# A state-space scan with a mixture of experts beside it: every second quad of scaled inputs kept in an accumulation bank

## The chip, the core and the metric

The kernel runs on one core of a Trainium2 chip. The metric is the time of one execution on the device, in microseconds (us), lower is better. Two runs of the kernel before stand beside each other in what follows: 1683.84 and 1686.05 us, with a median of 1684.94 us.

The engines are TensorE (PE, with its weight loads as PEld), VectorE (DVE), ScalarE (ACT), GpSimd (POOL) and the queue that issues most DMAs (SP). Each works through its own list of instructions in order; semaphores are what one waits for from another.

## The reference

`x` is 4 sequences of 1024 steps with 256 channels. After a layer norm two branches run on the same rows: a recurrent scan with 16 states for each channel, and a mixture of 8 experts (top 2, 1280 rows each at most) whose output gates the scan's. The scan is what matters here:

```
xn = layernorm(x)
dt = soft_clamp(softplus(xn @ Wdt.T + bdt), 0.001, 0.1, 0.5)
B, C = xn @ WB.T, xn @ WC.T
A = -exp(soft_clamp(A_log, -5, 5, 0.5))
dA = exp(soft_clamp(dt[..., None] * A, -8, 8, 0.5))      # decays
dB = dt[..., None] * B[:, :, None, :]
def step(h, ...):
    h = dAt * h + dBt * xt[..., None]                    # decayed state + scaled input
    h_norm = sqrt(sum(h * h, over all channels and states))
    h = h * min(20 / h_norm, 1)
    y = einsum(h, Ct) + Dp * xt
s = scan(step)                                           # 1024 steps, one after the other
out = x + s * silu(moe(xn))
```

## The kernel before

The state of one step is a tile of 128 partitions by 128 columns: a partition holds one of 4 sequences, 2 halves of the channels and 16 states, a column one of 128 channels. VectorE does the 1024 steps one after the other. The other engines prepare what a step needs, and do the mixture of experts in what time they have left.

**A step on VectorE** has seven instructions, here in the order in which they stand: `vv` = state times decay (L722); `mx`, the maximum with 1 of the square of the last norm (L725); the sum of `vv` times the scaled input (L728, a custom reduction, in the trace CUSTOM_DVE with a short accumulator read behind it); the sum of `vv` squared (L736, the same); the sum of both over the partitions (L740); the new state `hr`, which is `vv` times the last scale `sv` plus the scaled input (L751); and the next squared norm out of the sums and the scale (L755). Here and there one longer instruction of another chain (L618, L624, L641) stands between L740 and L751.

**GpSimd** raises `mx` to the power -1/2 (L531), which gives `sv`. L531 waits for L725 of the same step, and L751 waits for L531. After every 16th step GpSimd also multiplies 16 columns of scales (L538).

**Quads and blocks.** Work that prepares steps is done for a quad, which is 4 steps; 4 quads are a block (16 steps), and 4 blocks are a half (64 steps, 16 quads). Quads are numbered from 0 to 255. For quad q TensorE transposes four tiles of decays into one accumulation bank (L1170, `ps[0]` for even quads and `ps[1]` for odd ones), then spreads four tiles of inputs into another (L1176, always `ps[2]`), and behind them puts that quad's share of the experts' matmuls (L1188 up, L1204 down, L1115 turns). ScalarE copies the decays out to the ring `da` in SBUF (L952), writes the four inputs, scaled, to the ring `ur` in SBUF (L959, four instructions), then evicts the experts' results (L972, L976, L983) and computes the next half's decays (L858, L864) and the next halves' rates (L817 to L828).

Both rings have 32 slots, that is 8 quads. So ScalarE may be up to 8 quads ahead of VectorE; what holds it there is a wait at each block's start for the end of the block before the last (L942, on `q_ready`). VectorE, in the last step of a quad and ahead of L736, waits until the inputs of the next quad are written (`u_done`).

What each engine does in a quad is written out in the loops over `blk` and `q`; no scheduler changes the order. At a half's border ScalarE has far more to do than elsewhere: in the last quad of a half two decay exponentials (L864, 128x2048 each), in the first quad of the next half the windows of scales (L913), two more decay exponentials, and the softplus of a half that is still to come (L817 to L824).

## Time and profile before

| | |
|---|---|
| median of 2 runs | 1684.94 us (1683.84 to 1686.05) |
| span of the profiled execution | 1682.3 us |
| DVE busy | 1549.9 us, 92% |
| PE busy | 1305.2 us, 78% (PEld 1145.4 us) |
| ACT busy | 1211.1 us, 72% |
| POOL busy | 769.9 us, 46% |
| granted TensorE clock, mean | 0.874 of full speed |

The span goes from the first to the last instruction of the profiled execution. The page gives no time of that execution beside it; the two timed runs are 1.5 and 3.8 us longer than the span, which is what lies around it. The scan begins some 80 us after the start and its last step ends near 1657 us. From 350 to 1480 us the experts' matmuls run beside it.

### The profile page before, as it was taken

The numbers are of one execution on the slowest core, as the hardware profiler recorded it, in microseconds if no ns is written. First come the engines' busy times: TensorE is split into PE (matmuls) and PEld (weight loads), VectorE is DVE, ScalarE is ACT, GpSimd is POOL, SyncE is SP. The second block draws the span as 40 slices with busy tenths as digits, with TensorE's granted clock in tenths as the row PEclk, the third lists the DMA queues.
The fourth block names the chain that finished last, engine by engine and source line by source line (L and its number), as shares of the span: only waits on it lengthen the run. The fifth ranks groups of instructions, "written<-read, shape, count | busy, mean of one in ns | idle before, by whom it ended". The sixth has DMA issues, their size and how long they took to land.

```text
span 1682.3 us, 33906 instructions
## 1 busy us (share of the span) xinstructions
PE 1305.2 (78%) x9356; PEld 1145.4 (68%) x9356; DVE 1549.9 (92%) x9454; ACT 1211.1 (72%) x3142; POOL 769.9 (46%) x1254
## 2 busy tenths in 40 slices
PE   5864524398979898998989798898979799945661
PEld 5753424387868787787878687797868688834551
DVE  6688888899999999999999999999999989987788
ACT  3695737468877887868787877878777777947551
POOL 3156666543434444443434444343434334468852
PEclk8576767699989999999999999898999999967885
DMA  9941111210111021011002002011101210012245
GB/s 332 338 138 44 45 41 45 84 44 25 50 52 39 25 77 33 18 56 57 27 27 87 25 29 74 25 39 43 57 19 35 66 32 21 20 39 75 73 135 204
DMA packets 95532, 113.28 MB, mean 67 GB/s; under 512 B 8432, under 2 KB 85360, under 8 KB 95344
## 3 DMA queue, kind: packets, MB, share of 16 engines
q1 hardware_dynamic: 87696, 94.13, 17.4%
q0 software_dynamic: 6144, 16.79, 3.1%
q8 instruction: 74, 1.21, 0.3%
q14 instruction: 114, 0.93, 0.2%
q10 hardware_dynamic: 1504, 0.22, 0.1%
HBM read 60.91 MB, written 50.20 MB: 66 GB/s over the span
## 4 chain that ended last, share of the span: by engine, by line
PE 51%; ACT 15%; DVE 14%; POOL 7%; issue 7%; DMA 4%; SPq 1%; POOLq 0%; ACTq 0%; DVEq 0%
PE ps L1204 14%; PE ps L1188 13%; PE ps L1176 9%; PE ps L1170 5%; ACT arena L864 4%; POOL arena L531 4%; DVE arena L751 3%; POOL xg L511 3%; PE ps L1154 3%; PE ps L1138 3%; DVE arena L722 2%; DVE arena L728 2%; ACT arena L858 2%; DVE arena L740 2%; ACT arena L959 2%
## 5 line engine op out<-in xcount | busy, mean ns | idle before, releaser
L531 POOL TENSOR_TENSOR arena<-arena,neghalf 128x1 f32<-128x1 f32 x1025 | 591.3, 577 | 831.6 <-DVE arena L725 759.9
L751 DVE SCALAR_TENSOR_TENSOR arena<-arena 128x128 f32<-128x128 f32 x1024 | 362.6, 354 | 55.8 <-POOL arena L531 55.7
L1176 PE MATMUL ps<-arena,pick 128*128 128x128 f32 x2048 | 302.5, 295 | 48.7 <-ACT arena L959 28.3
L1188 PE MATMUL ps<-arena,wf 128*128 128x256 f32 x1280 | 309.6, 393 | 21.9 <-ACT arena L972 13.8
L1176 PEld LDWEIGHTS ps<-arena,pick 128*128 128x128 f32 x2048 | 279.3, 211 | 62.4 <-ACT arena L959 47.6
L959 ACT ACTIVATE arena<-ps,arena 128x128 f32<-128x128 f32 x1024 | 291.4, 376 | 30.5 <-PE ps L1176 28.8
L736 DVE CUSTOM_DVE_ANT_0 arena<-arena 128x128 f32<-128x128 f32 x1024 | 294.3, 287 | 8.0 <-PE ps L1138 6.5
L1204 PE MATMUL ps<-wp,arena 128*128 128x256 f32 x1280 | 297.3, 386 | 5.0 <-issue 2.7
L728 DVE CUSTOM_DVE_ANT_0 arena<-arena 128x128 f32<-128x128 f32 x1024 | 299.0, 292 | 0.0
L722 DVE TENSOR_TENSOR arena<-arena 128x128 f32<-128x128 f32 x1024 | 290.7, 284 | 0.0
L740 DVE TRANSPOSE_TENSOR_REDUCE arena<-arena 128x2 f32<-128x64 f32 x1024 | 251.3, 245 | 35.5
L1188 PEld LDWEIGHTS ps<-arena,wf 128*128 128x128 f32 x1280 | 245.1, 198 | 55.4 <-ACT arena L972 14.8
L858 ACT ACTIVATE arena<-arena,a16c,a 128x256 f32<-128x256 f32 x512 | 278.7, 609 | 0.1
L1204 PEld LDWEIGHTS ps<-wp,arena 128*128 128x128 f32 x1280 | 243.0, 195 | 36.7 <-issue 2.9
L1170 PE MATMUL ps<-ident,arena 128*128 128x128 f32 x1024 | 209.3, 331 | 59.6 <-ACT arena L864 58.8
L1170 PEld LDWEIGHTS ps<-ident,arena 128*128 128x128 f32 x1024 | 179.7, 244 | 89.0 <-ACT arena L864 64.8
L755 DVE TENSOR_TENSOR_SCAN arena<-arena 128x2 f32<-128x2 f32 x1024 | 221.1, 216 | 0.0
L952 ACT ACTIVATE arena<-ps 128x512 f32<-128x512 f32 x256 | 152.2, 595 | 70.8 <-PE ps L1170 61.4
L725 DVE TENSOR_SCALAR arena<-arena 128x1 f32<-128x1 f32 x1024 | 150.3, 147 | 0.0
L972 ACT ACTIVATE arena<-ps 128x512 f32<-128x512 f32 x160 | 95.4, 608 | 66.7 <-PE ps L1188 64.4
L913 ACT ACTIVATE arena<-arena,winmask 128x16 f32<-128x16 f32 x520 | 110.9, 316 | 21.2 <-POOL arena L538 21.0
L864 ACT ACTIVATE arena<-arena 128x2048 f32<-128x2048 f32 x64 | 119.0, 1907 | 0.2
(145 smaller groups left out, 1292.6 us busy)
## 6 DMA issues: line engine op xcount, KB each, us to landing
xg<-zeros SPq DMA_DIRECT2D x10, 1024.0 KB, 9.6
xrow<-xg SPq DMA_DIRECT2D x40, 256.0 KB, 2.8
yg<-arena SPq DMA_DIRECT2D x40, 256.0 KB, 2.2
arena<-in_x SPq DMA_DIRECT2D x16, 512.0 KB, 9.5
wf<-in_c_fc SPq DMA_DIRECT2D x8, 1024.0 KB, 5.0
wp<-in_c_proj SPq DMA_DIRECT2D x8, 1024.0 KB, 5.9
arena<-dx SPq DMA_DIRECT2D x66, 64.0 KB
ys<-arena SPq DMA_DIRECT2D x66, 64.0 KB
```

The costliest lines, as they stand in the source:

```text
L531: g.tensor_tensor(sv[:, slot, 1:2], mx, neghalf[:, 0:1], ALU.pow).then_inc(s_ready, 1)
L722: v.tensor_tensor(vv, hr[:, before, :], da[:, slot, :], ALU.mult).then_inc(v_ready, 1)
L728: v.tensor_tensor_reduce(out=junk[:, 0, :], in0=vv, in1=ur[:, slot, :], scale=2.0 / CLAMP ** 2, scalar=0.0, op0=ALU.mult, op1=ALU.add, acc ...
L736: v.tensor_tensor_reduce(out=junk[:, 1, :], in0=vv, in1=vv, scale=1.0 / CLAMP ** 2, scalar=0.0, op0=ALU.mult, op1=ALU.add, accum_out=ac[:, ...
L740: v.tensor_reduce(out=terms[:, slot, 0:2], in_=ac.unsqueeze(2).broadcast_to([P, 2, 32]), axis=AX.X, op=ALU.add, apply_transpose=True).then ...
L751: v.scalar_tensor_tensor(hr[:, slot, :], vv, sv[:, before, 1:2], ur[:, slot, :], ALU.mult, ALU.add)\
L858: last = a.activation(dst[:, :, k, n_, :], src[:, :, k, :], ACT.Tanh, scale=a16[:, c:c + 1], bias=a16c[:, c:c + 1])
L959: last = a.activation(ur[:, t + j, :], ps[2][:, j * P:(j + 1) * P], ACT.Copy, scale=terms[:, t + j, 3:4])
L1170: last = t.transpose(ps[q % 2][:, j * P:(j + 1) * P], tanhb[:, f, :, s], ident[:, :])
L1176: last = t.matmul(ps[2][:, j * P:(j + 1) * P], pick[:, q * QUAD + j, :], xin, start=True, stop=True)
L1188: last = t.matmul(ps[4 + j % 2][:, c * TS:(c + 1) * TS], wf[:, k, (2 * j + c) * P:(2 * j + c + 1) * P], xt[:, k, :], start=k == 0, stop=k ...
L1204: last = t.matmul(ps[7][:, j * D:(j + 1) * D], hid[:, k, j * P:(j + 1) * P], wp[:, k, :], start=k == 0, stop=k == FC - 1)
```

## The change

The scaled inputs of the even quads (slots 0 to 3, 8 to 11 and so on of the ring) are no longer written to `ur` in SBUF. ScalarE writes them into the accumulation bank `ps[1]`, and VectorE's L728 and L751 read them there. Odd quads stay in `ur`. Since the bank holds one quad, ScalarE waits, ahead of the first of the four writes of an even quad, until VectorE has done the last step of the even quad before it, two quads back: `h_ready` at `QUAD * quad + BLK - 3`, which is L751 of step 4q - 5. The bank is taken from the decays, which now all go through `ps[0]`; TensorE's transposes of a quad therefore wait until ScalarE has copied out the decays of the quad just before (earlier: two before). The lists of all five engines have the same instructions in the same order as before; what differs is where operands lie and two waits.

```diff
@@ names @@
+        def inputs_at(slot):
+
+            j = slot % QUAD
+            return ur[:, slot, :] if slot // QUAD % 2 else ps[1][:, j * P:(j + 1) * P]
@@ VectorE, each step @@
-                    v.tensor_tensor_reduce(out=junk[:, 0, :], in0=vv, in1=ur[:, slot, :], scale=2.0 / CLAMP ** 2, scalar=0.0,
+                    v.tensor_tensor_reduce(out=junk[:, 0, :], in0=vv, in1=inputs_at(slot), scale=2.0 / CLAMP ** 2, scalar=0.0,
...
-                    v.scalar_tensor_tensor(hr[:, slot, :], vv, sv[:, before, 1:2], ur[:, slot, :], ALU.mult, ALU.add)\
+                    v.scalar_tensor_tensor(hr[:, slot, :], vv, sv[:, before, 1:2], inputs_at(slot), ALU.mult, ALU.add)\
@@ ScalarE, before the loop @@
-            act.sem_inc(da_done, 2)
+            act.sem_inc(da_done, 1)
@@ ScalarE, each quad @@
-                    a.activation(da[:, t:t + QUAD, :].rearrange("p t d -> p (t d)"), ps[q % 2][:, :], ACT.Copy)\
+                    a.activation(da[:, t:t + QUAD, :].rearrange("p t d -> p (t d)"), ps[0][:, :], ACT.Copy)\
...
                     act.wait_ge(tu_ps, quad + 1)
+                    if q % 2 == 0 and quad >= 2:
+                        act.wait_ge(h_ready, QUAD * quad + BLK - 3)
                     for j in range(QUAD):
-                        last = a.activation(ur[:, t + j, :], ps[2][:, j * P:(j + 1) * P], ACT.Copy,
+                        last = a.activation(inputs_at(t + j), ps[2][:, j * P:(j + 1) * P], ACT.Copy,
@@ TensorE, each quad @@
-                        last = t.transpose(ps[q % 2][:, j * P:(j + 1) * P], tanhb[:, f, :, s], ident[:, :])
+                        last = t.transpose(ps[0][:, j * P:(j + 1) * P], tanhb[:, f, :, s], ident[:, :])
```

## Rows read from the trace of the kernel before

**Rows 1.** Groups by line: engine, operation, shapes, count | busy us, mean ns | idle before

```profile
L531 POOL TENSOR_TENSOR arena<-arena,neghalf 128x1 f32<-128x1 f32 x1025 | 591.3, 577 | 831.6 <-DVE arena L725 759.9 <-DMA xg<-arena,slot_of 25.0 <-DMA xg<-wf,slot_of 22.1
```

**Rows 2.** Timeline of DVE, one ordinary step: start us, length us, instruction

```profile
801.83 0.35 DVE L751 SCALAR_TENSOR_TENSOR arena<-arena 128x128 f32<-128x128 f32 x1
802.10 0.21 DVE L755 TENSOR_TENSOR_SCAN arena<-arena 128x2 f32<-128x2 f32 x1
...
802.45 0.14 DVE L725 TENSOR_SCALAR arena<-arena 128x1 f32<-128x1 f32 x1
802.56 0.29 DVE L728 CUSTOM_DVE_ANT_0 arena<-arena 128x128 f32<-128x128 f32 x1
...
803.11 0.25 DVE L740 TRANSPOSE_TENSOR_REDUCE arena<-arena 128x2 f32<-128x64 f32 x1
803.29 0.35 DVE L751 SCALAR_TENSOR_TENSOR arena<-arena 128x128 f32<-128x128 f32 x1
803.55 0.22 DVE L755 TENSOR_TENSOR_SCAN arena<-arena 128x2 f32<-128x2 f32 x1
```

**Rows 3.** Timeline of POOL, that step and the next

```profile
802.67 0.58 POOL L531 TENSOR_TENSOR arena<-arena,neghalf 128x1 f32<-128x1 f32 x1 [0.87 <-DVE arena L725]
...
804.77 0.22 POOL L538 TENSOR_TENSOR arena<-ccol,arena 128x16 f32<-128x16 f32 x1
```

**Rows 4.** Timeline of DVE, a first step of a block, beside L538

```profile
804.72 0.41 DVE L751 SCALAR_TENSOR_TENSOR arena<-arena 128x128 f32<-128x128 f32 x1
805.06 0.21 DVE L755 TENSOR_TENSOR_SCAN arena<-arena 128x2 f32<-128x2 f32 x1
```

**Rows 5.** Timeline of DVE, a step in which L736 had waited for ACT

```profile
98.45 0.25 DVE L740 TRANSPOSE_TENSOR_REDUCE arena<-arena 128x2 f32<-128x64 f32 x1
98.62 0.31 DVE L751 SCALAR_TENSOR_TENSOR arena<-arena 128x128 f32<-128x128 f32 x1
98.85 0.22 DVE L755 TENSOR_TENSOR_SCAN arena<-arena 128x2 f32<-128x2 f32 x1
```

**Rows 6.** Timeline of DVE and POOL, a step in which L531 began later

```profile
112.56 0.29 DVE L728 CUSTOM_DVE_ANT_0 arena<-arena 128x128 f32<-128x128 f32 x1
...
112.80 0.30 DVE L736 CUSTOM_DVE_ANT_0 arena<-arena 128x128 f32<-128x128 f32 x1
...
112.76 0.54 POOL L531 TENSOR_TENSOR arena<-arena,neghalf 128x1 f32<-128x1 f32 x1 [0.96 <-DMA xg<-wf,slot_of]
```

**Rows 7.** Groups by line of DVE in the routing, with and without an accumulation bank

```profile
L700 DVE TENSOR_TENSOR wp<-wp 128x512 f32<-128x512 f32 x1 | 0.7, 693 | 0.0
...
L701 DVE TENSOR_TENSOR wp<-wp,ps 128x512 f32<-128x512 f32 x1 | 0.7, 689 | 0.0
...
L675 DVE COPY arena<-ps 128x256 f32<-128x256 f32 x1 | 0.4, 425 | 4.9 <-PE ps L1051 4.9
...
L671 DVE CAST arena<-arena 128x256 f32<-128x256 int32 x1 | 0.3, 285 | 0.0
```

**Rows 8.** Timeline of ACT over a half's border, quads 78 to 81

```profile
565.45 1.14 ACT L959 ACTIVATE arena<-ps,arena 128x128 f32<-128x128 f32 x4
...
568.34 0.60 ACT L972 ACTIVATE arena<-ps 128x512 f32<-128x512 f32 x1 [1.13 <-PE ps L1188]
...
575.09 0.28 ACT L905 ACTIVATE arena<-ps 128x128 f32<-128x128 f32 x1 [2.21 <-PE ps L1121]
...
582.48 1.11 ACT L959 ACTIVATE arena<-ps,arena 128x128 f32<-128x128 f32 x4
...
592.93 1.11 ACT L959 ACTIVATE arena<-ps,arena 128x128 f32<-128x128 f32 x4
```

**Rows 9.** Timeline of DVE: L751 of step 307, L736 of step 323

```profile
573.85 0.32 DVE L751 SCALAR_TENSOR_TENSOR arena<-arena 128x128 f32<-128x128 f32 x1
...
596.85 0.29 DVE L736 CUSTOM_DVE_ANT_0 arena<-arena 128x128 f32<-128x128 f32 x1
```

**Rows 10.** Windows of 12 such borders (quads 46 to 225): length and busy time, summed

```profile
sum 345.94, PE 262.28 PEld 226.41 DVE 333.53 ACT 298.70 POOL 137.66; mean PE 21.86 PEld 18.87 DVE 27.79 ACT 24.89 POOL 11.47
```

## The prediction

> **What bounds the kernel now.** I read the groups by line first. VectorE is busy for 92% of the span and GpSimd for 46%, so VectorE looks like the bound. But L531, the power on GpSimd, stands out: 1025 times 577 ns, nearly all its idle time ahead of it ended by L725 on VectorE [rows 1]. So a step may be a loop through both engines, and the timeline decides.
>
> In an ordinary step L751 follows L751 after 1.46 us (801.83 to 803.29) [rows 2]. Through GpSimd the same stretch is: L751 to L755 0.27, L755 to L725 0.35, L725's start to L531's start 0.22, L531 0.58, and 0.04 from its end (803.25) to L751 [rows 2, 3]. That adds up to 1.46 us with nothing left over. VectorE's other instructions, L728, L736 and L740, run beside L531 and take almost as long. How much less is seen where ScalarE had delayed L736, so that the power was long there: L740 to L751 0.17 and L751 to L755 0.23, together 0.40 us [rows 5], against 0.44 in the ordinary step (803.11 to 803.55) [rows 2]. **So the loop through GpSimd paces the scan, and VectorE alone would need 0.04 us less, 1.41 us a step.** In the first step of a block L751 to L755 takes 0.34 us (804.72 to 805.06) [rows 4], 0.07 more than usual, while L538 runs on GpSimd (804.77 for 0.22) [rows 3].
>
> Then I read ScalarE, which must stay ahead of VectorE. On the whole it does, but not evenly. At a half's border it needs 28.59 us from the first input of quad 78 (565.45) to the last of quad 81 (592.93 + 1.11 = 594.04) [rows 8]. VectorE does four quads in some 23 us. In the kernel before, ScalarE has saved up a lead by then: it begins quad 78's inputs at 565.45 [rows 8], 8.7 us before VectorE has ended step 307 (573.85 + 0.32 = 574.17) [rows 9], and VectorE hardly ever waits. That lead is what the new wait takes.
>
> **The change, part by part.**
>
> *Reading the bank on VectorE.* L728 and L751 of 512 steps read their second input from an accumulation bank. No row before shows these two forms doing that. The nearest one is in the routing: the same two-input form with both inputs in SBUF takes 693 ns, and with the second in a bank 689 ns [rows 7]. By that row the read costs nothing. The far bound is a one-input form: a copy of 128x256 out of a bank takes 425 ns, a conversion of the same size inside SBUF 285 ns [rows 7]; the 140 ns for 256 columns would be 0.07 us for 128. I take nothing, since L701 has two inputs as L728 and L751 do.
>
> *GpSimd beside it.* L531 reads two columns from SBUF. It starts 0.11 us behind L728 in the ordinary step (802.56, 802.67) and takes 0.58 us [rows 2, 3]. Where it started 0.20 behind L728 (112.56, 112.76), it took 0.54 and L736 got a little longer instead, 0.30 [rows 6] against 0.29 [rows 9]. I read this as the two engines taking turns at something that a two-input VectorE instruction and GpSimd share, with L728 the one that makes L531 late by 0.04 us. With L728's second input in a bank, L531 should take 0.54.
>
> The loop through GpSimd then falls from 1.45 to 1.41 us in even quads, where VectorE alone stands as well, so no more than 0.04 comes out. GpSimd sends or fetches rows in 128 steps (12 to 138, every second one, and 930 to 993) and is late for other reasons there; leaving these stretches out, some 830 steps are ordinary, half of them in even quads: 415 x 0.04 = 16.6 us. The first step of every block lies in an even quad, and L751 no longer meets L538: 64 x 0.07 = 4.5 us. **Gain: 21 us.** The bounds are 0 (what L531 loses has another cause) and 21.
>
> *The wait on ScalarE.* An even quad's inputs may not be written before L751 of step 4q - 5. VectorE wants them ahead of L736 of step 4q - 1, four steps later. Three steps of 1.45 and the 0.6 us from the end of one L751 to the next L736 are 4.9 us; less the 1.1 us of the four writes, that leaves an on-time ScalarE a lead of some 4 us. Before, quad 78 had 8.7 us more. In ordinary quads this is enough, and the wait costs nothing, covered by VectorE's own steps. Behind the waiting write on ScalarE stand the evictions of the experts (L972, L983), the tanh pieces (L858) and the next decays (L952); TensorE then waits at L1176 of the next quad, since `ps[2]` isn't free, but not at that quad's expert matmuls.
>
> At a half's border it isn't enough. Quad 78's inputs start at 574.17 instead of 565.45, and quad 81's must be there at 596.85 [rows 9]: 22.68 us for what took 28.59. Some of the 28.59 goes: the 1.13 us that ScalarE waited for L1188 [rows 8], because TensorE does that work while ScalarE is held. The 2.21 us ahead of L905 [rows 8] should mostly stay, since those matmuls stand behind L1176 of quad 79, which needs quad 78's inputs out of `ps[2]`. So VectorE waits some 4.8 us here.
>
> Twelve such borders lie beside the experts' work. Together they take 345.94 us, and ScalarE is busy in 298.70 of them [rows 10]. VectorE's allowance is 12 x 22.68 = 272.2. VectorE idles for 345.94 - 333.53 = 12.4 us in them already, and I count some 5 of these, an estimate, as waits that give ScalarE more room: 277. **The loss is thus between 22 us (every wait of ScalarE for TensorE goes) and 69 us (none goes). I take the middle, 46.** In the windows the steps saved on VectorE are waited away again: 12 x 8 x 0.04 = 4 us of the gain.
>
> *Decays through one bank.* L1170 of a quad now waits until the decays of the quad before are copied out. That copy stands just ahead of the inputs of that quad, which L1176 behind L1170 waits for already; L1170 runs while ScalarE writes those. I take nothing; the bound is L1170's 0.8 us in a few quads at each border, which lies inside the 69.
>
> *Writing to a bank on ScalarE.* 512 of the 1024 writes of L959 end in a bank. No row has ScalarE do that; I take the same time. PSUM — Partial Sum Buffer in the Trainium skill, in its table of engine access under "Specifications (TRN2)", calls ScalarE faster to PSUM than to SBUF, and no run here shows it; it would shorten the border windows by less than a microsecond each.
>
> **The sum.** 1684.94 - 21 + 4 + 46 = 1714 us, 29 us above the median. The rows come from an execution with a span of 1682.3 us, 2.6 below the median; nothing of the difference lies in the scan's steps, so I add to the median.
>
> **The rivals.**
>
> *The relief doesn't come.* L531 stays at 0.58 because L728 isn't what delays it. For it: rows 6 stand beside a DMA issue of GpSimd's own, where more differs than the 0.09 us between the starts. Against: L736 grew just where L531 shrank. It keeps the loss alone: 1685 + 46 = 1731 us.
>
> *VectorE pays for the bank.* Both reads cost the far bound, 0.07 us. VectorE alone then needs 1.41 + 0.14 = 1.55 us, L531 is covered, and an even step is 0.10 longer: 512 x 0.10 = 51 us. The border windows grow by 0.8 us each, which takes 10 off the 46: 1685 + 51 + 36 = 1772 us. It decides from a cost of about 0.02 us for each read. Rows 7 speak against it. The Trainium skill speaks for it: VectorE: DVE Perf Modes, in the section on the TRN2 errata, puts VectorE's fixed cost at 120 cycles from PSUM and 58 from SBUF, an estimated 65 ns more per instruction at 0.96 GHz. By that rule the time would be near this rival's; where L701 and L700 can be compared, the trace doesn't agree.
>
> *ScalarE makes it up; not slower than before.* TensorE gets so far in the held time that ScalarE finds all its work ready at the border. Then the loss is 22 us at 12 borders, and with the gain of 17 the time is 1690 us. It decides from ScalarE's idle time in a border falling under 1 us from 3.9. Against it: the 2.21 us ahead of L905 hang on quad 79's L1176.
>
> *The wait never binds.* Then only the gain is left, 1664 us. The 8.7 us by which quad 78 would be held speak against it.
>
> **How the numbers follow.** Forecast (1700 to 1738 with the loss up to 69): 0.45. No relief: 0.22. VectorE pays: 0.12. ScalarE makes it up: 0.18. Never binds: 0.03. The range, 1684 to 1756 us, reaches from the third rival to part of the second, and leaves out the last and the worst of VectorE paying. Two per cent, about what a measurement here can tell from no change, is 34 us: over 1719 is slower. That holds 0.12 + 0.20 of the rivals and four tenths of the forecast, 0.50; faster than 1651 needs more than any term here gives, 0.03; the rest, 0.47, is within.
>
> **What would show it.** In the profile of the changed kernel L531's mean should fall to about 560 ns, with 540 in even quads; L728 and L751 out of a bank should be no longer than out of SBUF; ScalarE should wait for L751 ahead of its inputs, some 5 us in most even quads; and VectorE should wait for ScalarE ahead of L736, a few times in all, about 4 us each, at steps 195, 259, 323 and on by 64. I am wrong if VectorE's steps themselves get longer, if those waits are under 2 us, or if they come at other places, above all if TensorE, stopped again and again, falls behind and makes VectorE wait in the middle of halves.

## The result, and the profile after

The changed kernel takes 1750.85 us (1750.79 to 1750.9, 2 runs) against 1684.94. The ratio is 1.040 with a 95% interval of 1.0383 to 1.0417: it is 66 us slower. The forecast was 1714, also slower, but 37 us too low. Lines up to the new wait stand 5 further down than before (L531 is now L536, L728 L733, L736 L741, L751 L756, L864 L869), those behind it 7 (L959 is L966, L1176 L1183, L1138 L1145).

The head of the page of the changed kernel:

```profile
span 1749.0 us, 33970 instructions
...
PE 1344.7 (77%) x9356; PEld 1172.6 (67%) x9356; DVE 1529.6 (87%) x9454; ACT 1205.3 (69%) x3142; POOL 748.6 (43%) x1254
```

VectorE is busy for 20 us less than the 1549.9 of before and yet ends 67 us later. So what was added is waiting. Its groups by line of the changed kernel (count | busy us, mean ns | idle just before them, and what ended it) say where:

```profile
L741 DVE CUSTOM_DVE_ANT_0 arena<-arena 128x128 f32<-128x128 f32 x1024 | 295.0, 288 | 100.7 <-PE ps L1145 47.7 <-ACT arena L966 33.3 <-ACT ps L966 19.5
...
L756 DVE SCALAR_TENSOR_TENSOR arena<-arena 128x128 f32<-128x128 f32 x512 | 179.3, 350 | 27.1 <-POOL arena L536 27.1
L756 DVE SCALAR_TENSOR_TENSOR arena<-arena,ps 128x128 f32<-128x128 f32 x512 | 165.5, 323 | 23.0 <-POOL arena L536 23.0
...
L733 DVE CUSTOM_DVE_ANT_0 arena<-arena 128x128 f32<-128x128 f32 x512 | 149.6, 292 | 0.0
L733 DVE CUSTOM_DVE_ANT_0 arena<-arena,ps 128x128 f32<-128x128 f32 x512 | 146.9, 287 | 0.0
```

L741 is where VectorE waits for a quad's inputs (in the last step of the quad before, released by L966) and for the output products of L1145 (in the first step of a block). It idled there for 100.7 us. The same group of the kernel before:

```profile
L736 DVE CUSTOM_DVE_ANT_0 arena<-arena 128x128 f32<-128x128 f32 x1024 | 294.3, 287 | 8.0 <-PE ps L1138 6.5 <-ACT arena L959 1.5
```

So 92.7 us of waiting came, and of a time that is 66 us longer that leaves some 27 us for shorter steps. Counted from one L756 to the next, less the wait ahead of L741, the steps take 26 us less: 767.0 for 789.1 us in the even quads and 775.0 for 778.9 in the odd ones. The lines with "ps" behind "arena" are reads out of the bank. They aren't longer than those beside them (287 against 292 ns, 323 against 350).

The steps, in the timeline of VectorE of the changed kernel: two of an even quad, then two of an odd one.

```profile
799.76 0.32 DVE L756 SCALAR_TENSOR_TENSOR arena<-arena,ps 128x128 f32<-128x128 f32 x1
...
800.45 0.29 DVE L733 CUSTOM_DVE_ANT_0 arena<-arena,ps 128x128 f32<-128x128 f32 x1
...
801.15 0.32 DVE L756 SCALAR_TENSOR_TENSOR arena<-arena,ps 128x128 f32<-128x128 f32 x1
...
807.73 0.35 DVE L756 SCALAR_TENSOR_TENSOR arena<-arena 128x128 f32<-128x128 f32 x1
...
808.45 0.29 DVE L733 CUSTOM_DVE_ANT_0 arena<-arena 128x128 f32<-128x128 f32 x1
...
809.17 0.35 DVE L756 SCALAR_TENSOR_TENSOR arena<-arena 128x128 f32<-128x128 f32 x1
```

GpSimd in the same two steps:

```profile
800.55 0.54 POOL L536 TENSOR_TENSOR arena<-arena,neghalf 128x1 f32<-128x1 f32 x1 [0.86 <-DVE arena L730]
...
808.56 0.58 POOL L536 TENSOR_TENSOR arena<-arena,neghalf 128x1 f32<-128x1 f32 x1 [0.86 <-DVE arena L730]
```

The even step takes 1.39 us (799.76 to 801.15) and the odd one 1.44 (807.73 to 809.17); outside the first step of a block the medians of steps 140 to 930 are 1.40 and 1.44, and 1.44 for both before. The power L536 takes 0.54 beside a read from the bank and 0.58 beside one from SBUF, as in [rows 3] and [rows 6]. Its mean over all is 560 ns, where [rows 1] had 577.

Now the waits of the changed kernel (who waits for whom: us in total, times, longest):

```profile
ACT ps L966 <- DVE arena L756: 220.7, 66, 9.6
...
PE ps L1183 <- ACT ps L966: 132.6, 39, 9.9
...
DVE arena L741 <- PE ps L1145: 47.7, 15, 8.4
...
DVE arena L741 <- ACT arena L966: 33.3, 10, 5.2
...
DVE arena L741 <- ACT ps L966: 19.5, 11, 4.0
```

ScalarE is held 66 times, 3.3 us each on the mean, and TensorE behind it. The forecast had some 5 us in most of the 128 even quads, so there are fewer holds than it said, and they are shorter. Read step by step, VectorE's waits ahead of L741 lie where the forecast put most of them: 71.7 us at the twelve half borders (steps 63, 0 and 3 of the halves). Another 4.5 us lie inside halves (steps 271, 272 and 432), and 24.3 in the closing stretch (steps 959, 960, 976, 992, 1007, 1008). In the kernel before, it was 4.5 us at these borders, 1.9 in the closing stretch and 1.6 elsewhere.

ScalarE at the border of [rows 8], in the timeline of the changed kernel:

```profile
577.13 1.11 ACT L966 ACTIVATE ps<-ps,arena 128x128 f32<-128x128 f32 x4 [4.59 <-DVE arena L756]
578.14 1.10 ACT L979 ACTIVATE arena<-ps 128x512 f32<-128x512 f32 x2
...
582.83 0.60 ACT L979 ACTIVATE arena<-ps 128x512 f32<-128x512 f32 x1 [0.61 <-PE ps L1195]
583.34 0.60 ACT L983 ACTIVATE arena<-ps 128x512 f32<-128x512 f32 x1
586.15 0.28 ACT L910 ACTIVATE arena<-ps 128x128 f32<-128x128 f32 x1 [2.21 <-PE ps L1128]
...
593.54 1.08 ACT L966 ACTIVATE ps<-ps,arena 128x128 f32<-128x128 f32 x4
...
603.96 1.13 ACT L966 ACTIVATE arena<-ps,arena 128x128 f32<-128x128 f32 x4
```

It goes from 577.13 to 605.09, 27.96 us for 28.59 before. The 1.13 us ahead of quad 78's second eviction of up matmuls is gone (578.14), as forecast, but 0.61 us has come ahead of quad 79's (582.83), and the 2.21 ahead of L910 stays to the last digit. The windows of the same 12 borders (as [rows 10]):

```profile
sum 337.07, PE 248.66 PEld 211.90 DVE 259.45 ACT 296.96 POOL 108.25; mean PE 20.72 PEld 17.66 DVE 21.62 ACT 24.75 POOL 9.02
```

ScalarE's idle time in them went from 345.94 - 298.70 = 47.2 us to 337.07 - 296.96 = 40.1: **7 us in twelve borders**. VectorE's idle time in them went from 12.4 to 77.6.

### The profile page after: what moved, and what is told of

It reads as the page before. It is cut to its first block, busy times and chain, and to the rows that moved or that the text cites. A ratio compares the mean times of both kernels' runs of the same rounds, so it can differ in the third digit from the quotient of the medians.

```text
span 1749.0 us, 33970 instructions
## 1 busy us (share of the span) xinstructions
PE 1344.7 (77%) x9356; PEld 1172.6 (67%) x9356; DVE 1529.6 (87%) x9454; ACT 1205.3 (69%) x3142; POOL 748.6 (43%) x1254
## 4 chain that ended last, share of the span: by engine, by line
DVE 52%; PE 17%; ACT 12%; POOL 8%; issue 7%; DMA 3%; POOLq 0%; SPq 0%; ACTq 0%; DVEq 0%
DVE arena L756 10%; DVE arena L733 9%; DVE arena L745 8%; DVE arena L741 8%; DVE arena L727 7%; DVE arena L760 5%; ACT arena L869 4%; POOL arena L536 4%; PE ps L1211 3%; PE ps L1183 3%; POOL xg L516 3%; PE ps L1161 3%; DVE arena L730 2%; PE ps L1195 2%; PE ps L1177 2%
## 5 line engine op out<-in xcount | busy, mean ns | idle before, releaser
L536 POOL TENSOR_TENSOR arena<-arena,neghalf 128x1 f32<-128x1 f32 x1025 | 573.7, 560 | 919.3 <-DVE arena L730 848.3
L1183 PE MATMUL ps<-arena,pick 128*128 128x128 f32 x2048 | 328.7, 312 | 151.6 <-ACT ps L966 132.6
L1183 PEld LDWEIGHTS ps<-arena,pick 128*128 128x128 f32 x2048 | 298.4, 223 | 174.2 <-ACT ps L966 142.4
L741 DVE CUSTOM_DVE_ANT_0 arena<-arena 128x128 f32<-128x128 f32 x1024 | 295.0, 288 | 100.7 <-PE ps L1145 47.7
L1195 PE MATMUL ps<-arena,wf 128*128 128x256 f32 x1280 | 309.7, 393 | 25.6 <-issue 15.7
L966 ACT ACTIVATE ps<-ps,arena 128x128 f32<-128x128 f32 x512 | 141.8, 341 | 225.6 <-DVE arena L756 220.7
L1195 PEld LDWEIGHTS ps<-arena,wf 128*128 128x128 f32 x1280 | 245.2, 199 | 58.7 <-issue 16.9
L760 DVE TENSOR_TENSOR_SCAN arena<-arena 128x2 f32<-128x2 f32 x1024 | 221.7, 216 | 0.0
L756 DVE SCALAR_TENSOR_TENSOR arena<-arena 128x128 f32<-128x128 f32 x512 | 179.3, 350 | 27.1 <-POOL arena L536 27.1
L957 ACT ACTIVATE arena<-ps 128x512 f32<-128x512 f32 x256 | 153.4, 599 | 46.9 <-PE ps L1177 46.6
L756 DVE SCALAR_TENSOR_TENSOR arena<-arena,ps 128x128 f32<-128x128 f32 x512 | 165.5, 323 | 23.0 <-POOL arena L536 23.0
L966 ACT ACTIVATE arena<-ps,arena 128x128 f32<-128x128 f32 x512 | 147.5, 387 | 19.9 <-PE ps L1183 19.6
L733 DVE CUSTOM_DVE_ANT_0 arena<-arena 128x128 f32<-128x128 f32 x512 | 149.6, 292 | 0.0
L733 DVE CUSTOM_DVE_ANT_0 arena<-arena,ps 128x128 f32<-128x128 f32 x512 | 146.9, 287 | 0.0
```

The lines of the kernel that those rows point to most:

```text
L536: g.tensor_tensor(sv[:, slot, 1:2], mx, neghalf[:, 0:1], ALU.pow).then_inc(s_ready, 1)
L733: v.tensor_tensor_reduce(out=junk[:, 0, :], in0=vv, in1=inputs_at(slot), scale=2.0 / CLAMP ** 2, scalar=0.0, op0=ALU.mult, op1=ALU.add, ac ...
L741: v.tensor_tensor_reduce(out=junk[:, 1, :], in0=vv, in1=vv, scale=1.0 / CLAMP ** 2, scalar=0.0, op0=ALU.mult, op1=ALU.add, accum_out=ac[:, ...
L756: v.scalar_tensor_tensor(hr[:, slot, :], vv, sv[:, before, 1:2], inputs_at(slot), ALU.mult, ALU.add)\
L760: v.tensor_tensor_scan(horner, sv[:, before, 1:2].broadcast_to([P, 2]), terms[:, slot, 1:3], terms[:, slot, 0:1], ALU.mult, ALU.add).then_ ...
L966: last = a.activation(inputs_at(t + j), ps[2][:, j * P:(j + 1) * P], ACT.Copy, scale=terms[:, t + j, 3:4])
```

## The experiments

Each median stands beside that of the kernel before in the same runs (1682.8 to 1684.9 us). Line numbers differ by a few between kernels; those in the text are the changed kernel's where nothing else is said. "Idle" is VectorE's idle time ahead of L736 or L741 in the profiled execution, the number that was 8.0 before and 100.7 after. "Gain" is worked out: the kernel before's median, plus the idle time above 8.0, less the kernel's median. It is what must have come from shorter steps if nothing else changed. The idle time is that of one execution, whose time lies up to 4.6 us from the median of its kernel, so a gain is good to some 4 us.

| kernel | us | ratio, 95% interval | idle us | gain us |
|---|---|---|---|---|
| the change | 1750.85 | 1.0383 to 1.0417 | 100.7 | 26.8 |
| wait_alone | 1775.63 | 1.0494 to 1.0562 | 102.3 | 1.6 |
| one_bank_alone | 1683.04 | 0.9976 to 1.0005 | 7.3 | -0.8 |
| read_alone | 1676.56 | 0.9946 to 0.9971 | 21.2 | 19.6 |
| every_fourth | 1681.37 | 0.9986 to 1.0028 | 14.1 | 7.7 |
| no_bank_at_end | 1739.71 | 1.0311 to 1.0353 | 86.1 | 22.9 |
| wait_two_banks | 1757.55 | 1.0389 to 1.0450 | 86.0 | 5.0 |
| after_decays_later | 1749.10 | 1.0372 to 1.0411 | 96.3 | 23.7 |
| fourth_decays_later | 1695.11 | 1.0052 to 1.0107 | 30.7 | 12.1 |
| read_sum_only, read_state_only | 1678.08, 1681.71 | one run each | | |
| before_light | 1679.76 | 0.9962 to 0.9993 | 8.5 | 3.5 |
| after_light | 1735.76 | 1.0297 to 1.0331 | 84.1 | 23.1 |
| before_output_early | 1801.73 | 1.0678 to 1.0731 | 123.4 | -3.5 |
| after_output_early | 1804.14 | 1.0679 to 1.0743 | 150.4 | 21.1 |
| fourth_output_early | 1801.75 | 1.0689 to 1.0730 | 134.5 | 7.6 |
| after_turn_behind | 1746.77 | 1.0359 to 1.0400 | 92.1 | 20.2 |
| fourth_turn_behind | 1676.84 | 0.9955 to 0.9979 | 13.8 | 11.8 |

The last column sorts the kernels by how many quads read the bank, whatever else they do: half of them 20 to 27 us, a quarter 8 to 12, none -4 to 5. So, as far as that goes, the time is the kernel before's, less the relief, plus the waits ahead of this one line.

### One part at a time

**wait_alone**: the wait, with everything in SBUF as before.

```diff
                     act.wait_ge(tu_ps, quad + 1)
+                    if q % 2 == 0 and quad >= 2:
+                        act.wait_ge(h_ready, QUAD * quad + BLK - 3)
```

> The kernel before with only ScalarE's new wait ahead of the inputs of every even quad; inputs still go to SBUF and decays through two banks. Theory (the wait costs, the read gains): slower than the change itself, since the loss of some 93 us of VectorE's waiting stays and the shorter steps are missing: 1765 to 1785 us, with VectorE's waits ahead of L736 at 85 us or more. Rival (the loss comes from the decays in one bank): about 1685 us, VectorE waiting under 15 us. Rival (the bank traffic itself slows things): under 1740 us.

1775.63 us, 93 above the kernel before. The group of L736 in this kernel:

```profile
L736 DVE CUSTOM_DVE_ANT_0 arena<-arena 128x128 f32<-128x128 f32 x1024 | 294.6, 288 | 102.3 <-ACT arena L961 62.5 <-PE ps L1140 39.5
```

It waits as long as the changed kernel does, 102.3 against 100.7, with no bank read by VectorE and none taken from the decays. So the wait alone makes the loss, and all of it lands on this line. The read of the bank gives back what lies between this kernel and the change, 25 us.

**one_bank_alone**: the decays through `ps[0]` only.

```diff
-            act.sem_inc(da_done, 2)
+            act.sem_inc(da_done, 1)
...
-                    a.activation(da[:, t:t + QUAD, :].rearrange("p t d -> p (t d)"), ps[q % 2][:, :], ACT.Copy)\
+                    a.activation(da[:, t:t + QUAD, :].rearrange("p t d -> p (t d)"), ps[0][:, :], ACT.Copy)\
...
-                        last = t.transpose(ps[q % 2][:, j * P:(j + 1) * P], tanhb[:, f, :, s], ident[:, :])
+                        last = t.transpose(ps[0][:, j * P:(j + 1) * P], tanhb[:, f, :, s], ident[:, :])
```

> The kernel before with only the decays moved into one accumulation bank. Theory (the wait costs): 1680 to 1692 us. Rival (one bank makes TensorE late at the borders): 1700 us or more, with VectorE's waits ahead of L736 well above the 8 us of before.

1683.04 us, and 7.3 us of idle time where 8.0 were: no cost of it shows.

**read_alone**: the changed kernel without the wait. ScalarE writes all inputs to `ur`, and VectorE still reads the bank in even quads, whatever lies there.

```diff
-                    if q % 2 == 0 and quad >= 2:
-                        act.wait_ge(h_ready, QUAD * quad + BLK - 3)
                     for j in range(QUAD):
-                        last = a.activation(inputs_at(t + j), ps[2][:, j * P:(j + 1) * P], ACT.Copy,
+                        last = a.activation(ur[:, t + j, :], ps[2][:, j * P:(j + 1) * P], ACT.Copy,
```

> The change without ScalarE's wait: ScalarE writes all inputs to SBUF, and VectorE reads, in even quads, whatever lies in the bank, so the inputs of even quads are not the right ones; decays go through one bank. Theory (L531 is 0.04 us shorter where L728 reads a bank, no cost of the bank): 1655 to 1668 us, L531 at 538 ns in even quads, VectorE's waits ahead of L736 under 20 us. Rival (the gain is an effect of VectorE having waited for ScalarE): about 1685 us.

1676.56 us, only 6 us faster. The power has its relief (560 ns), but L741 idles more than before:

```profile
L741 DVE CUSTOM_DVE_ANT_0 arena<-arena 128x128 f32<-128x128 f32 x1024 | 294.5, 288 | 21.2 <-PE ps L1143 11.4 <-ACT arena L964 9.6
```

Of 20 us from shorter steps 13 are waited away, at the same half borders (3.84 us at step 640, 4.52 at 832, 2.82 at 451). So ScalarE and TensorE had only just kept up with the slower steps. The chain of the kernel before (the work that ended last, shares of the span), which the prediction didn't read, had it:

```profile
PE 51%; ACT 15%; DVE 14%; POOL 7%; issue 7%; DMA 4%; SPq 1%; POOLq 0%; ACTq 0%; DVEq 0%
```

Followed back from the last instruction, the path lay on TensorE and ScalarE for two thirds of the span, although VectorE was busy for 92% of it. In the changed kernel it lies on VectorE, which holds ScalarE again and again:

```profile
DVE 52%; PE 17%; ACT 12%; POOL 8%; issue 7%; DMA 3%; POOLq 0%; SPq 0%; ACTq 0%; DVEq 0%
```

**read_sum_only and read_state_only**: read_alone with the bank read by L733 only, and by L756 only. The first edit:

```diff
-                    v.scalar_tensor_tensor(hr[:, slot, :], vv, sv[:, before, 1:2], inputs_at(slot), ALU.mult, ALU.add)\
+                    v.scalar_tensor_tensor(hr[:, slot, :], vv, sv[:, before, 1:2], ur[:, slot, :], ALU.mult, ALU.add)\
```

> As read_alone (ScalarE writes all inputs to SBUF, no wait; VectorE reads what lies in the bank in even quads, so their inputs are not the right ones), but only the sum behind L728 reads the bank, and the new state (L751) reads SBUF. Theory (L728's second SBUF input is what delays L531): L531 at 538 ns in even quads, as with both; the first steps of blocks keep L751's 0.07 us beside L538. Rival (the state's read is what helps): L531 at 579 ns everywhere.

> As read_alone, but only the new state (L751) reads the bank in even quads (not the right inputs there). Theory: L531 stays at 579 ns, steps in even quads stay at 1.44 us, and only the first step of a block gets shorter, by some 0.06 us. Rival: even steps at 1.40 us.

The groups by line with the sum alone out of the bank:

```profile
L536 POOL TENSOR_TENSOR arena<-arena,neghalf 128x1 f32<-128x1 f32 x1025 | 575.7, 562 | 840.7 <-DVE arena L730 771.2
```

and with the state alone out of the bank:

```profile
L536 POOL TENSOR_TENSOR arena<-arena,neghalf 128x1 f32<-128x1 f32 x1025 | 591.7, 577 | 832.2 <-DVE arena L730 762.6
...
L756 DVE SCALAR_TENSOR_TENSOR arena<-arena,ps 128x128 f32<-128x128 f32 x512 | 177.0, 346 | 23.0 <-POOL arena L536 23.0
```

The first has the relief of L536 (562 ns), the second none (577, as before); what the second has is the first step of a block, 0.06 us shorter, as expected. It is L733's second input in SBUF, read while L536 runs, that makes L536 0.04 us longer.

### A longer lead, and loads taken off the border

**every_fourth**: the first quad of a block alone in the bank, so that ScalarE is held two quads later.

```diff
-            return ur[:, slot, :] if slot // QUAD % 2 else ps[1][:, j * P:(j + 1) * P]
+            return ur[:, slot, :] if slot // QUAD % 4 else ps[1][:, j * P:(j + 1) * P]
...
-                    if q % 2 == 0 and quad >= 2:
-                        act.wait_ge(h_ready, QUAD * quad + BLK - 3)
+                    if q == 0 and quad >= 4:
+                        act.wait_ge(h_ready, QUAD * quad + BLK - 11)
```

> The change, but only the first quad of each block goes into the bank, so that ScalarE waits for the end of the quad four back and may be some 15 us ahead instead of 4. Theory: nearly no waits of VectorE beyond those of before, and half of the read's gain, about 256 x 0.045 + 4 us: 1668 to 1678 us. Rival (any stop of ScalarE at that place costs what it did): 1700 us or more.

1681.37 us, no different from the kernel before. With two quads more of lead the idle time falls from 100.7 to 14.1. ScalarE is held at 8 of the 63 waits, 28.5 us in all, where the change holds it 66 times for 220.7: the loss is one of lead. Fewer waits and a longer lead come together in this edit, but the waits that are left seldom bind. Still, half the relief, less the 6 us waited away, leaves too little to measure, and the 1668 to 1678 expected isn't reached.

**wait_two_banks**: wait_alone, and the spread inputs go to `ps[2]` and the free `ps[1]` in turn, so that TensorE isn't stopped at L1176 by a held ScalarE.

```diff
+                        last = a.activation(ur[:, t + j, :], ps[1 + q % 2][:, j * P:(j + 1) * P], ACT.Copy,
...
-                    pe.wait_ge(u_done, quad + 1)
+                    if quad >= 1:
+                        pe.wait_ge(u_done, quad)
...
+                        last = t.matmul(ps[1 + q % 2][:, j * P:(j + 1) * P], pick[:, q * QUAD + j, :], xin, start=True, stop=True)
```

> The kernel before with ScalarE's new wait, decays in one bank, and TensorE's spread inputs alternating between the free bank and the old one, so that TensorE can go on for one more quad while ScalarE is held. Theory (much of the loss is TensorE being held at its next spread, not ScalarE): 1720 to 1745 us against 1775.6 with the wait alone. Rival (ScalarE's own burst sets the loss): 1765 us or more.

1757.55 us, between what the two theories gave. The loss falls from 93 to 73 and the idle time from 102.3 to 86.0: one more quad for TensorE is worth 16 to 20 us. TensorE isn't free in this kernel, though. Its stops behind the held writes, 157.7 us ahead of L1178 in wait_alone, are all but gone. But it now stops ahead of later transposes, until ScalarE has copied the decays out of the one bank, and that copy stands behind the held write:

```profile
PE ps L1172 <- ACT arena L952: 104.2, 28, 13.9
```

So this run doesn't show what is left of the loss when TensorE is never held.

**before_light and after_light**: half of the experts' matmuls left out in both kernels.

```diff
-                                for k in range(DH):
+                                for k in range(1):
...
-                            for k in range(FC):
+                            for k in range(FC // 2):
```

> The kernel before with half of the experts' matmuls left out (one of two pieces of the contraction of the up products, half of those of the down products), everything else in its place; the experts' output is not the right one. Theory (VectorE and GpSimd set the step, TensorE just keeps up): 1672 to 1684 us. Rival (TensorE sets much of the time already): under 1660 us.

> The change with the same half of the experts' matmuls left out. Theory (the loss is large because TensorE has no time to spare over a half, so what it idles while ScalarE is held never comes back): 1675 to 1715 us, the loss from VectorE's waits under half of the 100 us of the change. Rival (ScalarE's own burst at the borders sets the loss): 1730 us or more.

The kernel before gains 3 us (1679.76), and the changed one is still 56 us above it (1735.76). The chain of before_light lies on VectorE, where that of the kernel before lay on TensorE and ScalarE. Since the times are 3 us apart, the two paths are about equally long in the kernel before:

```profile
DVE 74%; POOL 7%; PE 7%; issue 6%; DMA 3%; ACT 1%; SPq 0%; POOLq 0%; DVEq 0%; ACTq 0%
```

The group of L741 in after_light, and below it its windows of the 12 borders:

```profile
L741 DVE CUSTOM_DVE_ANT_0 arena<-arena 128x128 f32<-128x128 f32 x1024 | 294.5, 288 | 84.1 <-ACT arena L966 44.1 <-PE ps L1145 28.7 <-ACT ps L966 11.1
```

```profile
sum 332.19, PE 209.09 PEld 174.60 DVE 258.85 ACT 297.54 POOL 107.76; mean PE 17.42 PEld 14.55 DVE 21.57 ACT 24.80 POOL 8.98
```

With 40 us less of TensorE's work in the windows (209.09 against 248.66) they are 5 us shorter, and ScalarE still idles for 332.19 - 297.54 = 34.7 us in them. My theory at this point was that TensorE, stopped behind ScalarE, has no time to spare; it fell. What ScalarE waits for there hangs for the most part on ScalarE itself. TensorE's timeline of the changed kernel shows it at the border above:

```profile
578.29 1.16 PE L1183 MATMUL ps<-arena,pick 128*128 128x128 f32 x8 [2.46 <-ACT ps L966]
579.29 3.50 PE L1195 MATMUL ps<-arena,wf 128*128 128x256 f32 x8
...
583.99 2.01 PE L1066 MATMUL ps<-arena 128*128 128x256 f32 x8 [0.69 <-ACT arena L983]
585.84 0.27 PE L1128 MATMUL ps<-ident,arena 128*128 128x128 f32 x1
589.70 1.16 PE L1177 MATMUL ps<-ident,arena 128*128 128x128 f32 x4 [3.59 <-ACT arena L869]
```

TensorE's work for quad 79 begins 2.46 us late, behind L966, which is held, so L1195 ends late for the eviction at 582.83. Then ScalarE empties a bank (L983), TensorE fills it again (L1066) and does L1128 behind that, and ScalarE's L910, the next in its list, waits 2.21 us for L1128, however late ScalarE came.

**no_bank_at_end**: quads from 236 on in SBUF and without the wait.

```diff
-            return ur[:, slot, :] if slot // QUAD % 2 else ps[1][:, j * P:(j + 1) * P]
+            return ur[:, slot, :] if quad % 2 or quad >= 236 else ps[1][:, j * P:(j + 1) * P]
...
-                    if q % 2 == 0 and quad >= 2:
+                    if q % 2 == 0 and 2 <= quad < 236:
```

> The change, but from quad 236 on all inputs go to SBUF again, without the new wait. Theory (the stretch of the expert combination, which the prediction left out, loses some 22 us because ScalarE loses its lead there too): 1727 to 1733 us against 1750.85 of the change, VectorE's waits ahead of L741 after step 950 back at some 3 us. Rival (those waits come from TensorE's work alone): about 1748 us.

1739.71 us: 11 us come back, for some 20 expected, and VectorE's waits in the closing stretch fall from 24.3 to 9.6 us. At steps 992 and 1008 it still waits 2.98 and 5.86 us. Why they stay isn't settled, but they aren't always the new wait's: in kernels without it the closing stretch waits between 1.9 us (the kernel before) and 12.4 (read_state_only).

**after_decays_later and fourth_decays_later**: the first quad's two decay pieces (L869) two quads later, in the changed kernel and in every_fourth.

```diff
-                    if blk % 4 == 0 and 0 < blk and q == 0:
+                    if blk % 4 == 0 and 0 < blk and q == 2:
                         for c in range(2, 4):
```

> The change, with the two decay exponentials that stand behind quad 16m's inputs moved two quads on, behind quad 16m+2's (a table load or two more). Theory (VectorE's waits at a half's border come from ScalarE's burst of 10 us between the inputs of quads 16m and 16m+1): each border loses some 3 us less, 1700 to 1725 us. Rival (the burst isn't what ends last; TensorE's output is): 1745 us or more.

> The first quad of each block in the bank, and the two decay exponentials moved two quads on. Theory (ScalarE and TensorE were just fast enough for the slower steps of before, and give a shorter step back as waits at the borders): the waits at borders go and the read's gain shows, 1668 to 1677 us. Rival (the gain of the read isn't there outside a held kernel): about 1683 us.

1749.10 and 1695.11 us, so no change that is clear of the noise, and 11 us more than the kernel before. The waits at step 3 of a half fall from 33 to 6.5 us, and steps 11, 15 and 16 wait 47 us in their place. ScalarE was also busy for longer, 1237.6 us for 1205.3, with 23 table loads for 13 ahead of L979. A burst that is moved by two quads delays the quads behind it.

**The output products.** At steps 640 and 832 VectorE waits 7.1 us each, more than anywhere else at the twelve borders. In the timeline of the changed kernel, first VectorE and then TensorE at the first of them:

```profile
1093.23 0.29 DVE L741 CUSTOM_DVE_ANT_0 arena<-arena 128x128 f32<-128x128 f32 x1 [4.00 <-ACT ps L966]
1101.86 0.30 DVE L741 CUSTOM_DVE_ANT_0 arena<-arena 128x128 f32<-128x128 f32 x1 [7.16 <-PE ps L1145]
```

```profile
1098.42 1.08 PE L1122 MATMUL ps<-ident,xrow 128*128 128x128 f32 x4 [5.36 <-ACT arena L824]
1099.30 0.63 PE L1141 MATMUL ps<-arena,ident 128*128 128x128 f32 x2
1099.86 1.92 PE L1145 MATMUL ps<-arena 128*32 128x128 f32 x32
```

VectorE waits for L1145, which stands behind a turn of the experts (L1122), which waits until ScalarE's softplus (L824) has freed its bank. In **after_output_early**, **fourth_output_early** and **before_output_early** the products stand right behind the first quad's inputs instead, ahead of all expert work; in **after_turn_behind** and **fourth_turn_behind** ahead of the turn alone, at quads 160 and 208. The first edit, and below it the second:

```diff
-                    if q == 1:
-                        output(blk, max(1, blk) * BLK + 1, blk % 2)
...
                     last.then_inc(tu_ps, 1)
+                    if q == 0:
+                        output(blk, max(1, blk) * BLK + 1, blk % 2)
```

```diff
-                    if q == 1:
+                    if q == 1 and not (blk % 4 == 0 and any(w[0] == "turn" for w in by_quad[quad - 1])):
                         output(blk, max(1, blk) * BLK + 1, blk % 2)
...
                         elif kind == "turn":
+                            if q == 0 and blk % 4 == 0:
+                                output(blk, max(1, blk) * BLK + 1, blk % 2)
```

> The change, with TensorE's output products of a block put ahead of the experts' work of the block's first quad instead of behind it. Theory (the 7 to 8 us waits at steps 640, 832 and 960 are the output standing behind the experts' turn, which waits for ScalarE's softplus): VectorE's waits for the output fall from 48 us to under 15; part of it comes back as waits for inputs of the next quad at the same borders: 1725 to 1740 us. Rival (all of it comes back, since ScalarE's burst ends as late as before): 1747 us or more.

> The first quad of each block in the bank, and TensorE's output products ahead of the experts' work of the block's first quad. Theory: of the 14 us of waits some 8 go, 1671 to 1678 us, a little faster than the kernel before. Rival (the shorter step is given back elsewhere): 1680 us or more.

> The kernel before with only the output products moved ahead of the experts' work. Theory (its waits for the output add up to 6.6 us, and the steps pace the rest): 1677 to 1682 us. Rival: no change, 1683 us.

> The change, with the output products ahead of the experts' turn in the first quads of two halves (quads 160 and 208) and nothing else moved. Theory (the 7 us waits at steps 640 and 832 are the output behind the turn, which waits for the softplus): these waits go to about 2 us, the step-643 and 835 waits for inputs come up to the 4 us of other borders: 1740 to 1746 us against 1750.85. Rival (the whole burst is late anyway): 1749 us or more.

> The first quad of each block in the bank, and the output ahead of the turn at quads 160 and 208. Theory: 3 to 5 us less waiting than the 14 of that kernel, 1675 to 1679 us, a little faster than the kernel before. Rival: 1681 us as without it.

The first three miss altogether: 1802 to 1804 us, whichever kernel. The waits of before_output_early say why:

```profile
PE ps L1134 <- ACT arena L913: 186.8, 63, 20.1
...
DVE arena L736 <- ACT arena L959: 123.4, 49, 6.1
```

The products begin with the windows of scales that ScalarE makes in the same quad (L913), so TensorE now stops for them in every block (63 times, 17 before), with the expert work queued behind. The other two are mild: after_turn_behind lies 4 us under the change, with overlapping intervals, since the 7.16 and 7.13 us are gone but 5.84 and 5.75 stand three steps on (643 and 835). fourth_turn_behind, at 1676.84, is the fastest kernel found that does the whole work, 0.3% under the kernel before; its waits are those of every_fourth (13.8 against 14.1 us), so whether the moved turn is what makes the difference to that one isn't shown.

## Why the prediction was wrong

The sum was -21 + 4 + 46 = 29 us. Measured, it is some -27 + 92.7 = 66. The time lies inside the stated range of 1684 to 1756 us, near the end where none of ScalarE's waits goes.

**The relief: right, with its mechanism.** L531 was to fall to 560 ns, 540 in even quads; it is 560, and 0.54 us. An even step gave up 0.05 us, where 0.04 was taken. L756 begins 65 ns behind the end of L536 there, for 35 in odd quads, so I read it as paced by VectorE alone since. In first steps of blocks L756 to L760 fell from 0.33 to 0.23 us, as in other even steps, so the 0.07 us beside L538 are gone too. read_sum_only against read_state_only shows that L728's input is the cause. The gain of 21 stands against 26 or 27 in the change and 20 to 24 in the other kernels with half of the quads in the bank.

**The bank costs VectorE nothing: right.** 287 against 292 ns for the sum; for the new state 346 against 351 in read_state_only, where L536 is as long in even quads as in odd ones. Nor does L741 begin later behind L733: a median of 213 ns in even quads, 218 in odd ones. The rule of VectorE: DVE Perf Modes in the Trainium skill (section on the TRN2 errata), 120 cycles from PSUM for 58, would have made both longer by an estimated 65 ns; in neither form here does the trace agree.

**Decays through one bank: right** (one_bank_alone, 1683.04). **ScalarE's writes to the bank** were taken at the same time. In the page of the changed kernel they are the shorter ones:

```profile
L966 ACT ACTIVATE ps<-ps,arena 128x128 f32<-128x128 f32 x512 | 141.8, 341 | 225.6 <-DVE arena L756 220.7
...
L966 ACT ACTIVATE arena<-ps,arena 128x128 f32<-128x128 f32 x512 | 147.5, 387 | 19.9 <-PE ps L1183 19.6
```

The even quads' writes took 373 ns on the mean before, so 341 is 32 ns less each. PSUM — Partial Sum Buffer in the Trainium skill ("Specifications (TRN2)") calls ScalarE faster to PSUM than to SBUF, and this trace agrees. It changes nothing in the time, since ScalarE is held just there.

**"In ordinary quads this is enough, and the wait costs nothing": right.** Inside halves VectorE waits for 4.5 us in all, and it waits at steps 195, 259 and 323 and on by 64, as forecast, though at some borders at steps 63 and 0 too. The forecast's own sign of failure, TensorE falling behind mid-half, isn't what happened.

**The step that failed: "I take the middle, 46."** The bounds were 22 (every wait of ScalarE for TensorE in the twelve border windows goes) and 69 (none goes), and the middle means that half of those 47.2 us go. Only 7.1 went. At the border of [rows 8] the 1.13 us went, by the forecast's reason: TensorE did that work in the held time. But TensorE was then late for quad 79, which the prediction didn't count, and 0.61 us came there. The 2.21 us stayed, but not because of quad 79's L1176, as it says: already in the kernel before, TensorE's work for L905 waits for L976, ScalarE's own instruction just ahead of it.

```profile
572.94 2.01 PE L1059 MATMUL ps<-arena 128*128 128x256 f32 x8 [1.03 <-ACT arena L976]
```

In all twelve windows, ScalarE's waits ahead of L905 went from 18.4 us to 16.2 (L910 in the changed kernel), those ahead of the up evictions L972 from 10.9 to 12.0 (L979), those ahead of the down evictions L983 from 11.5 to 9.9 (L990). I followed each wait back along TensorE to its last stop of over 0.3 us. In the changed kernel 27.0 of 38.7 us lead to a result of ScalarE (18.4 of them to L966); the other 11.7, at two borders, lead to a stop ahead of L1195 for which the trace names no releaser. Where it leads to ScalarE, a held ScalarE moves both, and the distance between them stays. after_light agrees: 34.7 us of waits remain with half the experts' matmuls gone. Then the allowance: I gave VectorE 5 us more room for old waits. Without them the rule of the prediction gives 337.07 - 272.2 = 65 us, and measured at the borders it is 71.7 - 4.5 = 67.2. So **the border term is 67 and not 46: 21 us**.

**And a part that was not costed: the closing stretch.** "Twelve such borders lie beside the experts' work" counted only those; the combination of the experts' outputs at steps 959 to 1008 is another place where ScalarE and TensorE need a lead, and VectorE waits 22 us more there. no_bank_at_end gives back 11 of them; that the rest is the new wait's isn't shown, since without it the stretch waits up to 12.4 us. Together with 2.9 more inside halves (4.5 for 1.6), the misses are 21.2 + 22.4 + 2.9 = 46.5, less 10 for a gain of 27 instead of 21 - 4 = 17. That is the 37 us between forecast and result.

**The rivals.** Two came as near as 20 and 21 us: "the relief doesn't come" at 1731 and "VectorE pays for the bank" at 1772. L536 excludes the first and L733 the second. "ScalarE makes it up" was to be told by ScalarE's idle time in a border falling under 1 us from 3.9; it fell to 3.3. "The wait never binds" is excluded by the 220.7 us of holds.

**What the experiments add.** The read alone is worth 6 us, not 21, because ScalarE and TensorE only just kept up. In a kernel that holds ScalarE anyway, the same 20 to 27 us come out whole (25 between wait_alone and the change). Of the loss of 93 us, one more quad for TensorE gives back 16 to 20 (wait_two_banks); half of the experts' matmuls less gives back 17 us of VectorE's waits (after_light). How the rest divides between ScalarE's own burst at a border and the hand-overs between the two engines stays open: ScalarE's 297 us of work in the windows alone are 25 above VectorE's 272, and the 40 of hand-overs move with it.

## What to carry to other kernels

A ring of buffers is also a store of lead, and a change that cuts it is costed at each place where the producer's burst is longer than the consumer's allowance, the closing stretch included. Take a producer's waits in a burst as staying until a row shows that what it waits for doesn't depend on the producer itself; here 40 of 47 us stayed. Before a faster step on the busiest engine is counted as a gain, read the chain that ended last: if it lies on other engines, the gain may turn into waits there, as 13 of 20 us did here. Its shares don't give the size, since two paths may be about equally long: half of the experts' matmuls less moved the chain from TensorE to VectorE and saved 3 us.

## What the runs showed of the hardware

The two-input sum L733 on VectorE makes the one-column power on GpSimd that runs beside it take 0.58 us when both of its inputs lie in SBUF, and 0.54 when one lies in an accumulation bank; which of the reads matters was settled only by read_sum_only. The sum of squares L741 also reads SBUF beside the power, in both cases; what it costs isn't shown. The new state's instruction, 323 ns instead of 350, didn't get shorter by its bank: with the bank but without the relief it takes 346, with the relief but out of SBUF a median of 322 (even quads of read_sum_only), and out of SBUF it took 0.31 us where the power was long there [rows 5]. In even steps of the changed kernel it begins a median of 65 ns behind the end of L536, in read_state_only 34.

Leaving out half of the experts' matmuls lowered the granted clock from 0.869 to 0.804 of full speed (mean of the span, after_light), and what was left got slower with it: an up matmul takes 439 ns instead of 393, one of L1183 334 instead of 312. At each of the two levels of the clock an up matmul takes the same in both kernels, 381 and 380 ns at 2.4 GHz and 619 and 627 at 1.2 GHz, but 152 of 640 begin at the lower level instead of 68 of 1280. So that experiment freed less of TensorE than it left out.
